# Gated cross-attention with a grouped mixture of experts: when the token tiles are gathered and scattered, and where the last chunk's second FFN products stand

## The reference, cut to what matters

```python
x = x + tanh(g_xattn) * (attention(layernorm(x), ctx, ctx) @ W.T + b)   # 16 heads, 77 keys
f = layernorm(x)
shared = swiglu(f @ w_in.T) @ w_out.T          # 256 -> 2 x 512 -> 256
h = swiglu(f @ w1.T)                           # first matrix of the experts, one for all tokens
routed = sum over the 2 chosen experts e of weight[e] * (h @ w2[e].T)
x = x + tanh(g_ffn) * (shared + routed)
```

## Time and profile before

| | |
|---|---|
| three executions, us | 1198.74, 1200.57, 1206.84 |
| profiled execution, us | 1195.1 |
| its span, us | 1193.2 |
| PE (TensorE matmul) busy | 1130.0 us, 95% |
| DVE (VectorE) busy | 803.1 us, 67% |
| ACT (ScalarE) busy | 469.8 us, 39% |
| POOL (GpSimd) busy | 439.7 us, 37% |
| mean granted TensorE clock | 0.985 |

### The profile page before, as it was taken

How to read it: one execution, slowest core, us unless ns; L and a number is a source line. 1 busy time by engine, 2 the same in 40 slices (tenths; PEclk the granted TensorE clock), 3 DMA queues, 4 the chain that set the end, 5 groups by cost and what they waited for, 6 DMA issues and landing times.

```text
span 1193.2 us, 22269 instructions
## 1 busy us (share of the span) xinstructions
PE 1130.0 (95%) x7475; PEld 902.7 (76%) x7475; DVE 803.1 (67%) x1777; ACT 469.8 (39%) x723; POOL 439.7 (37%) x576
## 2 busy tenths in 40 slices
PE   3979999999999999999999899999999699999997
PEld 1556877877776777777777677788888588888876
DVE  5566687677686786776777676446644488677776
ACT  4455555555555545545555432223322111111111
POOL 2122335235235335245334422200000466566653
PEclk9988999999999999999999999999999799999999
DMA  7976567647647647565764411478653555455441
GB/s 144 215 136 130 120 102 141 137 95 135 136 108 123 140 110 112 132 127 95 150 133 87 91 42 40 161 221 265 211 189 123 164 160 155 149 162 162 148 146 55
DMA packets 114721, 162.64 MB, mean 136 GB/s; under 512 B 37964, under 2 KB 79342, under 8 KB 114608
## 3 DMA queue, kind: packets, MB, share of 16 engines
q1 hardware_dynamic: 102964, 123.19, 45.8%
q0 software_dynamic: 11648, 38.03, 10.5%
HBM read 74.72 MB, written 51.58 MB: 106 GB/s over the span
## 4 chain that ended last, share of the span: by engine, by line
PE 76%; issue 10%; DVE 6%; POOL 4%; DMA 1%; ACT 1%; POOLq 0%; another core or an unknown queue 0%; DVEq 0%; ACTq 0%
PE ps L735 15%; PE ps L781 12%; PE ps L680 10%; PE ps L783 6%; PE ps L697 6%; PE ps L588 4%; PE ps L600 4%; PE ps L631 3%; PE ps L560 3%; PE ps L766 3%; PE ps L555 3%; POOL tab_dram L1410 2%; PE ps L583 1%; PE ps L609 1%; PE ps L654 1%
## 5 line engine op out<-in xcount | busy, mean ns | idle before, releaser
L781 PE MATMUL ps<-regr,gh 128*128 x600 | 221.4, 406 | 0.7 <-issue 0.7
L853 ACT ACTIVATE Pt<-ps,pbias 77x1024 f32<-77x1024 f32 x128 | 141.5, 1106 | 179.7 <-PE ps L588 172.9
L783 PE MATMUL ps<-regr,gl 128*128 x600 | 169.9, 283 | 0.6 <-issue 0.6
L1319 POOL DMA_INDIRECT yt<-y_dram,Pt x75 | 77.6, 1035 | 201.0 <-issue 200.7
L781 PEld LDWEIGHTS ps<-regr,gh 128*128 128x128 f32 x600 | 113.6, 189 | 24.4 <-issue 1.4
L1152 DVE TENSOR_REDUCE mneg<-ps 128x8 f32<-128x616 f32 x128 | 101.5, 794 | 45.4 <-PE ps L560 43.1
L945 ACT ACTIVATE gh<-ps 128x512 fp32r<-128x512 f32 x75 | 43.8, 598 | 209.1 <-PE ps L766 117.9
L783 PEld LDWEIGHTS ps<-regr,gl 128*128 128x128 f32 x600 | 113.8, 190 | 1.2 <-issue 1.1
L1386 POOL TENSOR_TENSOR x<-x,regf 128x512 f32<-128x512 f32 x32 | 41.1, 1286 | 193.5 <-DMA x<-in_x 193.5
L680 PE MATMUL ps<-x2h,winh 128*128 128x512 f32 x256 | 110.4, 431 | 0.5 <-DVE OHR L1060 0.5
L1423 POOL DMA_INDIRECT out<-ot,Pt x75 | 77.6, 1035 | 78.6 <-DVE ot L1278 44.4
(11 more groups left out here) (198 smaller groups left out, 2568.1 us busy)
## 6 DMA issues: line engine op xcount, KB each, us to landing
regr<-regr SPq DMA_DIRECT2D x96, 256.0 KB, 5.9
y_dram<-Pt SPq DMA_DIRECT2D x64, 256.0 KB, 2.2
regf<-in_x SPq DMA_DIRECT2D x32, 256.0 KB, 2.8
x<-in_x SPq DMA_DIRECT2D x32, 256.0 KB, 7.0
y_dram<-res SPq DMA_DIRECT2D x32, 256.0 KB, 2.1
regr<-regr SPq DMA_DIRECT2D x96, 77.0 KB, 4.8
x_dram<-x2h SPq DMA_DIRECT2D x14, 512.0 KB, 2.9
x_dram<-x2l SPq DMA_DIRECT2D x14, 512.0 KB, 3.7
```

The lines of the kernel that those rows point to most:

```text
L781: e.matmul(o, gh2[:, k % 3, fc, :], w2v[:, bass.ds(val, 1), fc, :, :].rearrange("p o h d -> p (o h) d"), start=fc == 0, stop=False, skip_g ...
L783: m = e.matmul(o[:, 0, :], gl2[:, k % 3, fc, :], w2v[:, bass.ds(val, 1), fc, 0, :].rearrange("p o d -> p (o d)"), start=False, stop=fc == ...
L853: e.activation(Pt[0:K, 4 * k:4 * k + 4, :].rearrange("k (n j) t -> k n (j t)", n=2), bank_of["sc", b, k][0:K, :, :], ACT.Exp, bias=pbias[: ...
L1319: e.indirect_dma_start(yt[k % RY][:, :], None, y, bass.IndirectOffsetOnAxis(ap=rt[:, k, 0:1].bitcast(I32), axis=0), bounds_check=NT, oob_i ...
```

## The change

Five edits:

1. In the list, the last chunk's eight second-product pieces (`ffn` 15, pieces 16 to 23) leave their place and are put behind the last `hid` stage. The rounding and the rest of its last 128 hidden features, which hung on piece 17, become a stage of their own, `last_gh`, in the old place.
2. GpSimd gathers tiles 0 and 1 in three parts each, of 256 columns. The two hidden parts wait for the stores of `hid` alone; the third parts, and whole tiles from 2 on, come after the wait for the stores of `res`. The third parts raise a semaphore `lr`, for which VectorE waits before it accumulates tile 0. The row numbers of the parts (3 row + part) are computed by three small GpSimd operations.
3. TensorE issues experts 0 ahead of turn 2.
4. In GpSimd's loop the scatter of tile k also waits until experts k+2 are done (for k up to 70), and the gather of tile k+8 until the first half of experts k+3 is done.
5. SyncE issues one more transfer at the start, from x to the third part of the last 512 rows of `y_dram` (512 KB), right behind the one on line 488; `clr` then counts six.

```diff
-CLR = 16 * 5
+CLR = 16 * 6
...
-    while at["ffn"] < 24 * NCH:
+    while at["ffn"] < 24 * NCH - 8:
         ffn(2)
+    order.append(("last_gh", NCH - 1, 0))
...
+    while at["ffn"] < 24 * NCH:
+        ffn(0)
     return order
...
                     e.dma_start(y[NT:NT + 1, :], ...).then_inc(s["clr"], 16)
+                    e.dma_start(y[NT - 2 * S:NT, 2 * D:3 * D], A["x"][NB - 2:NB].rearrange("b s d -> (b s) d")).then_inc(s["clr"], 16)
...
-                e.wait_ge(s[f"ly{k % RY}"], 16 * (k // RY + 1))
+                e.wait_ge(s[f"ly{k % RY}"], 16 * (k // RY + 1 + (k % RY < 2)))
...
             for k in range(NTILE):
+                if k == 0:
+                    experts(k)
                 if k + 2 < NTILE:
                     turn(k + 2)
-                experts(k)
+                if k:
+                    experts(k)
...
+                if k == 0:
+                    e.wait_ge(s["lr"], 32)
...
+            def gather_part(k, j):
+                e.indirect_dma_start(yt[k % RY][:, j * D:(j + 1) * D], None, y3,
+                                     bass.IndirectOffsetOnAxis(ap=ix[:, j, k:k + 1], axis=0),
+                                     bounds_check=3 * NT + 2, oob_is_err=True).then_inc(s["lr" if j == 2 else f"ly{k % RY}"], 16)
...
+            e.wait_ge(s["rc"], 16 * NTILE)
+            for j in range(3):
+                e.tensor_scalar(ix[:, j, :], rt[:, 0:2, 0].bitcast(I32), 3, j, ALU.mult, ALU.add).then_inc(s["ix"], 1)
+            e.wait_ge(s["ix"], 3)
+            for n in range(4):
+                e.wait_ge(s[f"hd{n}"], 16 * NCH)
+            for k in range(2):
+                for j in range(2):
+                    gather_part(k, j)
             for n in range(2):
                 e.wait_ge(s[f"yr{n}"], 16 * NCH)
-            for n in range(4):
-                e.wait_ge(s[f"hd{n}"], 16 * NCH)
-            e.wait_ge(s["rc"], 16 * NTILE)
-            for k in range(RY):
+            gather(2)
+            gather(3)
+            gather_part(0, 2)
+            gather_part(1, 2)
+            for k in range(4, RY):
                 gather(k)
             for k in range(NTILE):
+                if k + 4 < NTILE:
+                    e.wait_ge(s["ex"], 2 * (k + 2) + 2)
                 e.wait_ge(s["acc1"], 2 * k + 2)
...
                 if k + RY < NTILE:
+                    e.wait_ge(s["ex"], 2 * (k + 3) + 1)
                     gather(k + RY)
```

More of the change, by code:

```diff
@@ L198, in build @@
         y = nc.dram_tensor("y_dram", (NT + 1, YD), F, kind="Internal").ap()
+        y3 = y.rearrange("n (k d) -> (n k) d", k=3)
         xd = nc.dram_tensor("x2_dram", (NCH - 2, 2, P, 2, 512), F, kind="Internal").ap()
@@ L375, in build @@
         ti = stage[0:1, 3984:4096].bitcast(I32)[:, 0:NTILE]
+        ix = stage[:, 3232:3238].bitcast(I32).rearrange("p (j k) -> p j k", j=3)
         ei = stage[0:1, 3072:3072 + 2 * NTILE].bitcast(I32).rearrange("p (t k) -> p t k", k=2)
@@ L810, in split, with high @@
                     e.activation(w2v[:, x - 4, :, 0, :], w2r[:, x - 4, :, 1, :], ACT.Copy).then_inc(s["wh"], 1)
+            def high(b, fc):
+                n = 4 * b + fc
+                e.wait_ge(s["f"], n + 1)
+                if b >= 1:
+                    e.wait_ge(s["so"], 2 * b)
+                e.activation(gh[:, fc, :], gf[:, n % 2, :], ACT.Copy).then_inc(s["gh"], 1)
             for stage_, b, k in order:
@@ L894, in scalar @@
                         e.activation(tt[:, n % 2, :], bank_of["ha", b, fc][:, :], ACT.Tanh, scale=0.5).then_inc(s["t"], 1)
[L895 to L900, removed]
+                    if 1 <= fc < 5 and part == 1 and (b, fc) != (NCH - 1, 4):
+                        high(b, fc - 1)
+                elif stage_ == "last_gh":
+                    high(b, 3)
                 elif stage_ == "route" and k == R_EXP1:
@@ L1321, in gather, with low @@
                                      bounds_check=NT, oob_is_err=True).then_inc(s[f"ly{k % RY}"], 16)
+            def gather_part(k, j):
+                e.indirect_dma_start(yt[k % RY][:, j * D:(j + 1) * D], None, y3,
+                                     bass.IndirectOffsetOnAxis(ap=ix[:, j, k:k + 1], axis=0),
+                                     bounds_check=3 * NT + 2, oob_is_err=True).then_inc(s["lr" if j == 2 else f"ly{k % RY}"], 16)
+            def low(b, fc):
+                n = 4 * b + fc
+                e.wait_ge(s["gh"], n + 1)
+                e.tensor_tensor(gl[:, fc, :], gf[:, n % 2, :], gh[:, fc, :].bitcast(F), ALU.subtract).then_inc(s["gl"], 1)
             def root(n, b):
@@ L1389, in gpsimd @@
                     fc, part = k // 4, k % 4
[L1390 to L1393, removed]
+                    if 1 <= fc < 5 and part == 1 and (b, fc) != (NCH - 1, 4):
+                        low(b, fc - 1)
+                elif stage_ == "last_gh":
+                    low(b, 3)
                 elif stage_ == "route":
```

## The result

The changed kernel took 1187.95 us (median of 4, 1185.24 to 1189.21), the kernel before 1202.72 (median of 4: the three of the table above and 1204.87): a ratio of 0.9866, 95% interval 0.9825 to 0.9907. That is 14.8 us less, about twice the 7.5 of the forecast. The time of 1187.95 lies inside the forecast's range of 1184 to 1202. The two profiled executions differ by only half of that: 1195.1 and 1187.66, spans 1193.2 and 1185.5.

A forecast was written before the change was run, and what follows sets the result against it. TensorE, 95% busy, was taken as the bound, with time only in gaps and lower-clock stretches. Terms -6.8 (gap), -1.7 (pacing) and +1.0 (extra transfer) gave -7.5: 1200.57 became 1193.1, predicted 1193, range 1184 to 1202.

The forecast's parts named there:

- My own lower bound: Part gathers at the gap: latency at least 3.5 us, the whole gather's 4.38 less 0.9 for missing bytes.
- the upper bound of 2.5: Extra 512 KB transfer at the start: at most 2.5 us lost, 0.52 MB at 213 GB/s, all on TensorE's path.
- the mis-sized term: Pacing in the expert tiles: 1.7 us gained, half of 3.45, with bounds of 3.45 gained or lost.
- (b): Expert tiles: pacing also removes losses of timed executions not in the profile; 1186, some way to 1183; chance 0.17.
- the lost 3.45 us: Last 11 expert tiles up to turn 74: they take 39.16 us instead of 35.71, in waits put down to "issue".
- the sum of -7.5: Whole kernel: 6.8 gained up to experts 1, 1.7 by pacing, 1.0 lost to the extra transfer.
- 0.23 for faster by over 1%: Whole kernel: chance of a time under 1188.6 us; same had 0.72, slower by over 1% 0.05.
- (a): Expert tiles: the pacing does nothing, only bubble and gap are gained; -5.8 us, 1194.8; chance 0.20.
- (c): Gap before the expert tiles: gain stays there, part gathers late or start loses 2.5 us; -1 or so, 1199; chance 0.11.
- (d): Steady expert tiles, turn k+8: gathers late, over 7.9 us; 0.5 us over in each of 67 gives 1226; chance 0.07.

The follow-up runs named there:

- e5: The changed kernel itself, timed again on the slow chip: 1188.9 us against 1202.3 for the kernel before, ratio 0.989.
- e7: The kernel before plus only the extra 512 KB transfer at the start, on the slow chip: 1202.9 us against 1202.3, ratio 1.0005.
- e6: The changed kernel without the pacing, on the slow chip: 1205.2 us against 1202.3 for the kernel before, ratio 1.0025.
- e2: The kernel before plus only the pacing, on the first quick chip: 1190.9 us against 1190.5, ratio 1.000.
- e12: The kernel before plus only the pacing, again, on the second quick chip: 1191.5 us against 1189.8, ratio 1.0009.
- e1: The changed kernel without the pacing, on the first quick chip: 1185.3 us against 1190.5 for the kernel before, ratio 0.995.

## Why the prediction was right, and what it missed

**Edit 1, the move: right.** 1.56 us of waiting gone and the end of the first-matrix products predicted at 918.65; they ended at 918.31 (916.76 and 1.55). The second products ran from 918.15 to 924.1 without a wait, 5.76 us of work as counted. How well the times agree is in part luck: in e5's profile of the same kernel these products began at 921.41.

**Edit 2, the parts: right in order, short in one size.** First part predicted at 922.47, was 922.03. I gave a part 3.5 to 4.4 us to arrive; it took 2.99 (923.47 to 926.46) and 2.97 (926.13 to 929.10). So turn 0 came at 926.46, before the predicted 927.4 to 928.3. The Trainium skill's line for such a gather ("DMA: Bandwidth & Descriptors", anatomy of one DMA) gave 0.6 us less than a whole one; the trace shows 1.4 less (4.38 and 2.99). The trace does not agree with that difference, and the measurement decides. My own lower bound took off 0.9 for the missing bytes, 0.5 too little.

**Experts 0: too hopeful.** I gave them 2.81 to 4.38 us. They took 5.17 (930.32 to 935.49): though the idle time ahead fell from 8.2 us to 2.4 and 2.0, the clock was at its lower level for nearly all of them. The early parts and the slow experts 0 offset each other, which is luck: experts 1 at 936.28, in 935.3 to 937.5, a gain of 6.96 for 6.8.

**Edit 5: charged 1.0, nothing shows in the profile.** The first-matrix tiles began at 749.84 where the old first products had ended at 750.18. e7 gave 1.0005, with an interval that leaves room for the 1.0 and for the upper bound of 2.5.

**Edit 4, the pacing: the mis-sized term.** I took 1.7, between -3.45 and +3.45. In the profiled pair it was 0.45, on quick chips 0, on the slow chip 16.3 between e6 and e5 (17.1 by the turns of their profiles). The step that failed is the one that bounded this term by the one profiled execution: "Bounds are therefore a gain of 3.45". I had noted that the three timed executions lay 3.6 to 11.7 us above the profiled one, and had put this into rival (b), at 0.17, with the argument that nothing showed its place. (b) is the case that came, 1186 forecast and 1187.95 measured. Its premise, losses of the same kind, is what the traces bear out: the short waits around 1142 and 1156 us, among the lost 3.45 us of the profiled execution, are the beat that fills the tiles of e6 and half of those of e7. The kernel before with the pacing alone on the slow chip would have tested it directly, and wasn't run. So the time is in the range, but the sum of -7.5 is not what brought it there. The size of the loss in timed runs was there to read; only its place wasn't. The same miss is in the chances: 0.23 for faster by over 1%, and the measured ratio is 0.9866.

**Rivals (a), (c), (d).** (a), that the pacing does nothing, is true on the quick chips (e2, e12) and false on the slow one. (c) fell with the part gathers' 2.99 us. (d), late gathers, did not come in force: one turn of the changed kernel waits for its rows by the trace, 0.70 us at 1129.48, the first of its kind after more than 50 tiles.

## What to carry to other kernels

Work that fills a gap and a transfer that may start without it are one edit: on a quick chip each alone gave nothing (1.0 us faster, 2.3 slower), both 5.2. On the slow chip even both gave nothing until the transfers behind them were paced (e6). When timed executions lie several us above the profiled one, treat that as a term of the sum with unknown place, and not as noise. And an edit that steadies the issue of transfers has to be timed on more than one chip: taking it out cost 16 us on one, and adding it gave nothing on two.

## What the runs showed of the hardware

The same kernel took 1190.5, 1189.8 and 1202.3 us on three chips of one type, at the same granted clock of 1.00 in the expert tiles. Most of the difference lies in those tiles: by the turns, 11.6 us in e7's profile and none in e2's and e12's. In e6 the slow chip's TensorE stands 16 times, 14.3 us apart, in waits put down to "issue". The trace counts the transfers of the instruction queue in the stretch 945 to 1165 us, first e6, then e1 (queue, packets, MB, share):

```profile
q8 instruction: 13, 0.21, 0.4%
```

```profile
q8 instruction: 15, 0.25, 0.5%
```

That is 16 KB a packet, one in 17 and in 15 us. The Trainium skill ("Runtime: NRT & Kernel Launch", instruction fetch mechanics) says that instructions come in blocks of 16 KiB and that this is mostly hidden. The size agrees. The spacing of the waits is near that of the blocks, and TensorE stands where the program has no wait, which makes late instructions a candidate, against the page's rule.

The trace of e6 speaks against these packets as the cause. The 14 of them from 952.44 to 1165.28 are 16.4 us apart and the waits of TensorE 14.3, so they drift past each other: the first wait, at 962.83, comes 10.4 us behind a packet, the seventh, at 1049.83, 2.0 us ahead of one (1051.85). The program being fixed, a block that holds an engine up should stand at one distance from the wait. Nor are they slower: a packet takes 0.9 to 1.4 us in e6 and 0.9 to 1.6 in e1, where with as many packets nothing waits. What keeps the beat stays open.
